# Ranking split around the first operands, bias rows over all partitions, residual transposes one step later, addresses in registers

## The chip, the cores and the metric

The kernel runs on one core of a Trainium2 chip. The metric is the device time of one execution in microseconds (us). The engines of the core are TensorE (PE in the profile, with its weight loads as PEld), VectorE (DVE), ScalarE (ACT), GpSimd (POOL) and SyncE (SP), which here only issues DMAs. They run side by side and are ordered by semaphores alone.

## What is computed

32 sequences of 64 tokens, 512 wide, go through four layers: a transformer-like block without mask (single-head attention with scores over the sequence, a projection, two MLPs, the residual, a clip to 0..1), an adapter (down to 256, GELU, up to 512, residual, layer norm, gain and shift), and both once more with other weights. The adapter's weights are chosen per sequence by its role.

```python
# block (layers 0 and 2)
q = x @ Wq; k = x @ Wk; v = x @ Wv
attn = softmax(einsum('btd,bTd->btT', q, k) * scale)
attn_out = einsum('btT,bTd->btd', attn, v) @ Wp + bp
cms_out = gelu(attn_out @ cW1 + cb1) @ cW2 + cb2 + one_hot(target_codes)
modifier = gelu(concatenate([attn_out, cms_out]) @ mW1 + mb1) @ mW2 + mb2
out = clip(x + cms_out + modifier, 0.0, 1.0)
# adapter (layers 1 and 3)
h = gelu(einsum('bsh,bhk->bsk', hidden_states, W_down[role]) + b_down[role])
y = hidden_states + einsum('bsk,bkh->bsh', h, W_up[role]) + b_up[role]
out = (y - mean) * rsqrt(var + 1e-5) * gamma[role] + beta[role]
```

## The kernel before

All matmuls are float32 split into a high and a low part: ACT makes the high part by a rounding copy (`... HI ...`), DVE the low part by a subtraction (`minus`, L1146), and PE adds three products (`product`, L543). Each engine's program is written out by hand in order; what follows is that order.

**Start.** Wq with Wk, and Wv with Wp, are multiplied once per layer, four products n = 0..3 (`operands(n)` splits their inputs, `results(n)` their outputs into `fw`). Products 0 and 1 arrive in chunks, 2 and 3 reuse the buffers. The outputs of 0 and 1 are stored to DRAM (`fused`, L352 on SP) before ACT may overwrite them with those of 2 and 3. DVE also ranks the batches by role (`rank_batches`, 40 small steps on tiles `rk` and `rc`, counted by the semaphore `ranked`), so that two sequences of one tile mostly have the same role; SP waits for the ranking, reads each batch number from the tile `order` into a register (L341) and loads x (`load_x`, L342). On DVE the ranking stands behind `operands(1)` and ahead of `operands(2)`. POOL splits the adapters' bias rows meanwhile (L482 to L488, tiles `rows_hi`, `rows_part`, `rows_raw`, `rows`), on four partitions, two per layer, where a sign per partition taken from the ranking's `rc` picks high or low part.

**Passes.** The tokens go in 2 halves of 16 sequences, each through 2 layers: passes p = 0..3. A pass is attention in two blocks of 512 tokens, the MLPs in 16 units, and the adapter over 8 tiles of 128 tokens. Only the last tile of the second half may mix two roles (`general`) and takes its products twice.

**Adapter.** Per tile i: DVE clips `acc` into `xc` (`clip`, L1504, two buffers), ACT and DVE split it (`split_x`), PE multiplies down (`front`, L795, bias row L798) and at its end transposes the residual into the bank of the up-projection (L803), after waiting for `yn_done` of tile i-3; ACT makes the GELU, PE transposes it (`turn_h`, L816), ACT and DVE split it (`split_h`), PE multiplies up on top of the residual (`adapter_up`, L828, L831). DVE takes the row statistics (L1526, L1529, L1531), POOL the power for the deviation (L523), DVE normalises into `yt` (L1541), POOL multiplies by the gain and adds the shift (L526, L528), which SP loads per tile with an address read per sequence (L358, two DMAs of 64 partitions). In layer 0 PE transposes y back (`turn_back`, L840) and ACT copies it to x; in layer 1 SP stores it (L387), again with an address read each, and loads the next half's x between. PE's step i is front(i+2), turn_h(i+1), turn_back(i-2), adapter_up(i). Tile 5's turn_back stands at the end of the pass, those of tiles 6 and 7 inside the next attention, behind its second and fourth product. The adapter's weights are split by `adapter_part` and `up_part` (three roles each) around the end of the last MLP unit, where DVE also makes the last quadrant (`make_z12`) and the last sums (`add`, L1394).

## Time and profile before

| | us |
|---|---|
| median of 3 runs | 2183.42 (2183.08 to 2183.86) |
| the profiled execution | 2183.24 |
| its span in the trace | 2181.4 |

| engine | busy us | share of the span |
|---|---|---|
| PE | 2094.2 | 96% |
| DVE | 1417.4 | 65% |
| ACT | 864.6 | 40% |
| POOL | 378.1 | 17% |

### The profile page before, as it was taken

How to read it: one execution, taken by the hardware profiler on the slowest of the kernel's cores; microseconds unless marked ns; L12 is line 12 of the kernel's file. 1: busy time of each engine (PE TensorE's matmuls, PEld its weight loads, DVE VectorE, ACT ScalarE, POOL GpSimd, SP SyncE). 2: the span in 40 equal slices, each digit the busy share in tenths (PEclk: the TensorE clock that was granted, in tenths of full speed). 3: DMA queues.
4: the chain of work that ended last, by engine and by line, in shares of the span. 5: the costliest groups of instructions: out<-in, count | busy, mean ns of one | idle time of the engine just before them, and what ended most of it. 6: DMA issues, size and time to landing. Idle time of an engine off the chain costs nothing.

```text
span 2181.4 us, 27070 instructions
## 1 busy us (share of the span) xinstructions
PE 2094.2 (96%) x9640; PEld 1729.3 (79%) x9640; DVE 1417.4 (65%) x2228; ACT 864.6 (40%) x1492; POOL 378.1 (17%) x348
## 2 busy tenths in 40 slices
PE   5999999999799999999889999999989999999996
PEld 4888888887688888888768888888867888888874
DVE  8577786557558777556646777765555777865563
ACT  4454453333245444333325444333324544433331
POOL 3011112210311102111130110212122111112204
PEclk8999999999999999999999999999999999999998
DMA  4501111223320121112451111111332012111123
GB/s 174 234 30 58 49 63 58 68 68 97 131 78 30 58 80 37 68 68 68 152 157 39 49 59 66 65 60 52 107 121 102 20 49 68 68 46 60 65 92 97
DMA packets 42402, 169.74 MB, mean 78 GB/s; under 512 B 5648, under 2 KB 9744, under 8 KB 34832
## 3 DMA queue, kind: packets, MB, share of 16 engines
q1 hardware_dynamic: 42272, 168.02, 22.7%
q8 instruction: 80, 1.31, 0.2%
q14 instruction: 50, 0.41, 0.1%
HBM read 146.99 MB, written 21.01 MB: 77 GB/s over the span
## 4 chain that ended last, share of the span: by engine, by line
PE 87%; DVE 6%; SPq 2%; issue 2%; ACT 1%; POOL 1%; DMA 1%; DVEq 0%; ACTq 0%; POOLq 0%
PE psum L543 80%; PE psum L828 1%; PE psum L640 1%; DVE acc L1394 1%; PE psum L618 1%; DVE yt L1541 1%; PE psum L803 1%; PE psum L795 1%; DVE xz L1146 1%; DVE stats L1526 1%; DVE fpart L1146 0%; ACT xz L1095 0%; DVE wup L1146 0%; PE psum L831 0%; POOL yt L526 0%
## 5 line engine op out<-in xcount | busy, mean ns | idle before, releaser
L543 PE MATMUL psum<-hs,wd 128*128 128x512 f32 x3072 | 718.2, 389 | 5.6 <-DVE acc L1394 5.6
L543 PEld LDWEIGHTS psum<-hs,wd 128*128 128x128 f32 x3072 | 576.1, 188 | 128.1 <-DVE acc L1394 7.3
L1394 DVE TENSOR_TENSOR acc<-psum,acc 128x512 f32<-128x512 f32 x448 | 291.0, 682 | 101.4 <-PE psum L543 101.2
L543 PE MATMUL psum<-cop,wsm 128*128 128x512 f32 x1416 | 354.7, 389 | 0.0
L543 PE MATMUL psum<-aop,wsm 128*128 128x512 f32 x1320 | 332.9, 389 | 0.0
L543 PE MATMUL psum<-aop,wsc 128*128 128x512 f32 x1320 | 310.7, 389 | 0.0
L543 PEld LDWEIGHTS psum<-cop,wsm 128*128 128x128 f32 x1416 | 265.8, 188 | 55.1
L543 PEld LDWEIGHTS psum<-aop,wsm 128*128 128x128 f32 x1320 | 247.8, 188 | 51.4
L543 PEld LDWEIGHTS psum<-aop,wsc 128*128 128x128 f32 x1320 | 247.5, 188 | 51.3
L1008 ACT ACTIVATE hs<-psum,bias 128x512 fp32r<-128x512 f32 x88 | 60.8, 691 | 445.4 <-PE psum L543 445.3
L1146 DVE TENSOR_TENSOR hs<-zt,hs 128x512 fp32r<-128x512 f32 x256 | 179.9, 703 | 85.5 <-ACT zt L1009 85.5
L1008 ACT ACTIVATE hs<-zt,bias 128x512 fp32r<-128x512 f32 x168 | 120.5, 717 | 229.1 <-DVE zt L1376 173.1
L1369 DVE TENSOR_TENSOR zt<-psum,zt 128x512 f32<-128x512 f32 x56 | 38.7, 692 | 184.5 <-PE psum L543 184.5
L1009 ACT ACTIVATE zt<-zt,bias 128x512 f32<-128x512 f32 x168 | 119.0, 708 | 0.0
L497 POOL TENSOR_TENSOR comb<-w1m 128x512 f32<-128x512 f32 x28 | 36.2, 1292 | 476.7 <-DMA w1m<-m_in 476.7
L1146 DVE TENSOR_TENSOR wsm<-w1m,wsm 128x512 fp32r<-128x512 f32 x156 | 107.9, 711 | 0.0
L543 PE MATMUL psum<-fw,xs 128*128 128x512 f32 x384 | 97.2, 406 | 4.7 <-DVE tq L1146 3.4
L978 ACT ACTIVATE wsm<-w1m 128x512 fp32r<-128x512 f32 x156 | 93.9, 623 | 3.7 <-POOL w1m L504 3.7
L501 POOL TENSOR_TENSOR comb<-comb,w1m 128x512 f32<-128x512 f32 x28 | 48.9, 1746 | 249.6 <-DVE wsm L1146 249.6
L497 POOL TENSOR_TENSOR comb<-w1c 128x256 f32<-128x256 f32 x28 | 20.7, 740 | 408.8 <-DMA w1c<-c_in 408.8
L543 PE MATMUL psum<-xs,fw 128*128 128x512 f32 x384 | 90.7, 395 | 0.4 <-DVE xs L1146 0.4
L543 PEld LDWEIGHTS psum<-fw,xs 128*128 128x128 f32 x384 | 73.1, 195 | 20.8 <-DVE tq L1146 3.9
(169 smaller groups left out, 2439.6 us busy)
## 6 DMA issues: line engine op xcount, KB each, us to landing
w1m<-m_in SPq DMA_DIRECT2D x32, 1024.0 KB, 4.9
w1c<-c_in SPq DMA_DIRECT2D x32, 512.0 KB, 3.5
w<-c_in SPq DMA_DIRECT2D x32, 512.0 KB, 3.5
w<-m_in SPq DMA_DIRECT2D x32, 512.0 KB, 3.5
gains<-roles_in SPq DMA_DIRECT2D x64, 256.0 KB, 3.6
fw<-fused SPq DMA_DIRECT2D x6, 2048.0 KB, 10.0
fused<-fw SPq DMA_DIRECT2D x4, 2048.0 KB, 8.2
xmid<-x SPq DMA_DIRECT2D x4, 2048.0 KB, 6.7
```

The lines of the kernel that those rows point to most:

```text
L497: nc.gpsimd.tensor_tensor(st, w_block(u, 1, 0), w_block(u, 1, 1), ALU.add).then_inc(s1_made, 1)
L501: nc.gpsimd.tensor_tensor(st, st, w_block(u, 0, 0), ALU.subtract).then_inc(s2_made, 1)
L543: mm = nc.tensor.matmul(out, lhs(a), rhs(b), start=(start and n == 0), stop=(stop and n == total - 1), skip_group_check=reopened)
L618: nc.tensor.matmul(out, tq[:, j // 2, HI, j % 2, i * P:(i + 1) * P], xs[:, :, j, tile], start=(j == 0), stop=False)
L640: nc.tensor.matmul(out, val[:, HI, v_cols], val[:, :, p_cols], start=True, stop=False)
L795: nc.tensor.matmul(out, tokens, wdn_flat[:, bass.ds(role * (2 * KC * BN) + (c * KC + k) * BN, BN)], start=(b == 0 and k == 0 and a == c), ...
L978: nc.scalar.activation(slot(u, i)[:, HI, :], w_source(u, i), ACT.Copy).then_inc(s_hi[i], 1)
L1008: nc.scalar.activation(hs[:, b, HI, m, :], h_source(h, u), ACT.Gelu, bias=b1)
L1009: nc.scalar.activation(h_raw(h), h_source(h, u), ACT.Gelu, bias=b1).then_inc(h_hi[h], 1)
L1146: return nc.vector.tensor_tensor(out, a, hi.bitcast(F32), ALU.subtract)
L1369: nc.vector.tensor_tensor(zt[:, 2, :], bank_b()[:, :], zt[:, 0, :], ALU.add).then_inc(u3_done, 1)
L1394: nc.vector.tensor_tensor(dst, d_out[o][:, :], dst, ALU.add).then_inc(acc_done, 1)
```

## The change

It has these parts.

- The ranking is cut in two: `compare_batches` (before the first operands) and `place_batches` (behind the second); the two steps for the sign and the one for parity of the partition are gone (37 steps for 40). The ids are loaded from ACT's queue, no longer SP's. The one-hot tile `oh` is built behind `results(3)`.
- The bias rows lie over all 128 partitions, 36 elements each, high and low part beside each other; POOL has two instructions for four, and SP stores them in four DMAs.
- PE's residual transposes are a step of their own, `residual(p, i+1)` behind `turn_h(i+1)`, and wait for `yn_done` of tile i-2; `xc` has a third buffer (`xct2`).
- `up_part(1)` and `up_part(2)`, `clip(0)`, `add` and `adapter_part(2)` change places around the end of the last unit.
- turn_back of tiles 5, 6, 7 stands in the next attention, behind products 0, 2 and 3.
- SP reads each batch number once per half and keeps it in a register; the gains of a tile of one role come in one DMA over 128 partitions.

```diff
-            sp.dma_start(ids[:, :], ids_in).then_inc(ids_loaded, 16)
...
             sp.wait_ge(ranked, RANKED)
+            sp.nop(nofuse=True)
+            where = []
             for j in range(NB):
-                load_x(0, j)
-            sp.wait_ge(rows_made, 4)
-            sp.dma_start(brows, rows[:, :].bitcast(F32)).then_inc(rows_stored, 16)
+                where.append(batch(0, j))
+                load_x(where[j], j)
+            sp.wait_ge(rows_made, 2)
+            for layer in range(LAYERS):
+                for part in range(2):
+                    half_rows = slice(layer * P // LAYERS, (layer + 1) * P // LAYERS)
+                    sp.dma_start(brows[layer, part].rearrange("(q n) -> q n", n=RW),
+                                 rows[half_rows, part, :].bitcast(F32)).then_inc(rows_stored, 16)
...
             def load_gains(half, layer, i):
                 sp.nop(nofuse=True)
-                for b in range(2):
+                pieces = 1 + general(half, i)
+                for b in range(pieces):
...
-            nc.gpsimd.tensor_copy(rows_hi[:, :], rows_raw[:, :]).then_inc(rows_made, 1)
+            nc.gpsimd.tensor_copy(rows[:, HI, :], rows_raw[:, :]).then_inc(rows_made, 1)
             pool.wait_ge(rows_made, 1)
-            pool.wait_ge(ranked, 3)
-            nc.gpsimd.tensor_scalar(rows_part[:, :], rows_hi[:, :].bitcast(F32), rc[0:2 * LAYERS, 1:2], None, ALU.mult).then_inc(rows_made, 1)
-            nc.gpsimd.tensor_scalar(rows_raw[:, :], rows_raw[:, :], rc[0:2 * LAYERS, 0:1], None, ALU.mult).then_inc(rows_made, 1)
-            pool.wait_ge(rows_made, 3)
-            nc.gpsimd.tensor_tensor(rows[:, :], rows_raw[:, :], rows_part[:, :], ALU.add).then_inc(rows_made, 1)
+            nc.gpsimd.tensor_tensor(rows[:, LO, :], rows_raw[:, :], rows[:, HI, :].bitcast(F32), ALU.subtract).then_inc(rows_made, 1)
...
+            def residual(p, i):
+                if i == 2:
+                    pe.wait_ge(acc_done, 8 * UNITS * (p + 1))
                 if i >= 3:
-                    pe.wait_ge(yn_done, e - 2)
+                    pe.wait_ge(yn_done, 8 * p + i - 2)
...
                         if i + 1 < TILES:
                             turn_h(p, i + 1)
+                            residual(p, i + 1)
                         if layer == 0 and 2 <= i < TILES - 1:
                             turn_back(p, half, i - 2)
                         adapter_up(p, half, i, r.pop(i))
-                    if layer == 0:
-                        turn_back(p, half, TILES - 3)
...
                     add(p, layer, last, 0, *range(KC))
-                    adapter_part(p, 2)
                     dve.wait_ge(xadd_done, NG * (p + 1))
                     dve.wait_ge(acc_done, 8 * UNITS * (p + 1) - 4)
                     clip(0)
+                    adapter_part(p, 2)
+                    split_x(0)
                     clip(1)
-                    split_x(0)
-                    up_part(p, 2)
+                    up_part(p, 1)
                     add(p, layer, last, 1, 0)
                     split_x(1)
-                    add(p, layer, last, 1, 1, 2, 3)
+                    dve.wait_ge(dn_done, 8 * UNITS * (p + 1))
                     clip(2)
                     split_x(2)
+                    up_part(p, 2)
                     split_h(0)
+                    add(p, layer, last, 1, 1, 2, 3)
```

DVE's program at the start, before (`fpart` are the split operands, `rk` and `rc` the ranking's tiles, `idf` the ids as floats):

```order
L1146 TENSOR_TENSOR fpart_61<-fraw_57,fpart_61 128x512 x8
L1146 TENSOR_TENSOR fpart_97<-fraw_80,fpart_97 128x512 x8
L1191 TENSOR_SCALAR rk<-odds,pcol 128x16
L1193 TENSOR_REDUCE rc<-rk 128x1
L1198 TENSOR_SCALAR rc<-rc 128x1
L1199 TENSOR_SCALAR rk<-srow,pcol 128x32
L1201 CAST idf<-ids 128x65
L1203 TENSOR_SCALAR rk<-idf 128x32
```

and in the changed kernel:

```order
L1203 TENSOR_SCALAR rk<-srow,pcol 128x32
L1205 CAST idf<-ids 128x65
L1207 TENSOR_SCALAR rk<-idf 128x32
L1208 TENSOR_SCALAR rk<-idf 128x32
L1210 TENSOR_TENSOR rk<-rk 128x32
L1211 TENSOR_REDUCE rc<-rk 128x1
L1212 TENSOR_REDUCE rc<-rk 128x1
L1214 TENSOR_REDUCE rc<-rk 128x1
L1215 TENSOR_SCALAR rk<-odds,rc 128x16
L1217 TENSOR_REDUCE rc<-rk 128x1
L1158 TENSOR_TENSOR fpart_61<-fraw_57,fpart_61 128x512 x8
L1158 TENSOR_TENSOR fpart_96<-fraw_79,fpart_96 128x512 x8
```

Ten steps of the ranking have moved ahead of the operands and three are gone.

PE's program in a tile of layer 0, from the end of the down-projection to the up-projection (`brow` bias rows, `xct` the clipped tile, `hgt` the GELU's output, `yt` the normalised tile), before:

```order
L798 MATMUL psum<-brow,onz 128x256
L803 MATMUL psum<-ident,xct 128x128 x4
L816 MATMUL psum<-ident,hgt 128x128 x2
L840 MATMUL psum<-ident,yt 128x128 x4
L828 REGISTER_ALU
L828 MATMUL psum<-wup,hz 128x512
```

and in the changed kernel:

```order
L806 MATMUL psum<-brow,onz 128x256
L828 MATMUL psum<-ident,hgt 128x128 x2
L816 MATMUL psum<-ident,xct 128x128 x4
L852 MATMUL psum<-ident,yt 128x128 x4
L840 REGISTER_ALU
L840 MATMUL psum<-wup,hz 128x512
```

The transposes of `xct` stand behind those of `hgt`, and belong to the tile before the one whose down-projection has just run.

SP's program in pass 1, the gains and the first store of a tile, before:

```order
L357 TENSOR_LOAD roles
L357 ISA x2
L358 ISA
L358 DMA gains<-roles_in 64x1024
L357 TENSOR_LOAD roles
L357 ISA x2
L358 ISA
L358 DMA gains<-roles_in 64x1024
L386 TENSOR_LOAD order
L386 ISA x2
L387 ISA
L387 DMA out<-yt 64x512
```

and in the changed kernel, the gains, both stores and the first loads of x:

```order
L370 TENSOR_LOAD roles
L370 ISA x2
L371 ISA
L371 DMA gains<-roles_in 128x1024
L397 DMA out<-yt 64x512 x2
L347 ISA
L347 DMA x<-x_in 128x256
L347 ISA
L347 DMA x<-x_in 128x256
```

One address read is left per tile, that of the gains; the stores and the loads of x have none.

## Rows read from the trace of the kernel before

**Rows 1.** Busy time by stretch: stretch, length, busy us (instructions) per engine, PEclk, DMA.
```profile
0.00:75.00 75.00, 51.44 (x216) 42.49 (x217) 53.40 (x82) 26.08 (x37) 22.04 (x21) 0.86 0.56 201
528.00:608.60 80.60, 68.06 (x348) 53.55 (x346) 46.51 (x82) 25.90 (x48) 26.47 (x25) 0.96 0.28 99
1051.00:1156.10 105.10, 86.97 (x432) 68.74 (x431) 55.66 (x106) 32.36 (x61) 25.84 (x25) 0.94 0.44 146
1580.00:1660.60 80.60, 70.35 (x365) 54.91 (x364) 45.82 (x81) 25.51 (x48) 27.24 (x27) 0.98 0.28 99
2103.00:2181.40 78.40, 55.74 (x286) 42.46 (x284) 39.69 (x75) 17.40 (x33) 25.97 (x26) 0.91 0.26 74
```

**Rows 2.** The same view, behind PE's long gap at the start.
```profile
51.40:60.00 8.60, 8.59 (x30) 7.00 (x31) 8.46 (x9) 0.00 (x0) 0.00 (x0) 0.78 0.39 112
```

**Rows 3.** Waits of PE, whole span: total us, times, longest us.
```profile
PE psum L803 <- DVE yt L1541: 30.5, 18, 1.9
...
PE psum L543 <- DVE acc L1394: 5.6, 4, 1.4
```

**Rows 4.** Timeline of the start: start us, us, engine, instruction, count, idle before.
```profile
21.81 6.11 POOL L485 TENSOR_SCALAR rows_part<-rows_hi,rc 4x2304 f32<-4x2304 f32 x1 [1.88 <-DVE rk L1199]
21.90 6.06 DVE L1203 TENSOR_SCALAR rk<-idf 128x32 f32<-128x32 f32 x1
...
34.40 4.74 DVE L1213 TENSOR_TENSOR rc<-rc 128x1 f32<-128x1 f32 x1
...
44.28 0.21 DVE L1188 STREAM_TRANSPOSE codes<-rk 128x32 f32<-128x32 f32 x1
...
46.18 4.48 DVE L1146 TENSOR_TENSOR fpart<-fraw,fpart 128x2048 fp32r<-128x2048 f32 x2
...
51.41 8.81 PE L543 MATMUL psum<-fpart 128*128 128x512 f32 x30 [20.89 <-DVE fw L1146]
```

**Rows 5.** Timeline before the first attention, SP and ACT.
```profile
63.33 15.88 SPq L352 DMA_DIRECT2D fused<-fw  x4
70.85 2.07 ACT L882 ACTIVATE fw<-psum 128x512 fp32r<-128x512 f32 x4 [34.64 <-DMA fused<-fw]
```

**Rows 6.** Timeline of pass 0's adapter: before its first tile, then one tile.
```profile
531.11 2.36 DVE L1146 TENSOR_TENSOR wup<-raw_u,wup 128x1024 fp32r<-128x1024 f32 x2 [0.18 <-ACT wup L1042]
...
568.08 0.70 DVE L1526 BATCH_NORM_STATS2 stats<-psum 128x6 f32<-128x512 f32 x1 [1.42 <-PE psum L831]
...
569.17 0.42 DVE L1504 TENSOR_SCALAR xct<-acc 128x512 f32<-128x512 f32 x1
...
570.89 0.80 DVE L1541 TENSOR_SCALAR yt<-psum,mv,rstd 128x512 f32<-128x512 f32 x1
571.75 0.66 PE L803 MATMUL psum<-ident,xct 128*128 128x128 f32 x4 [1.77 <-DVE yt L1541]
...
573.19 1.30 POOL L528 TENSOR_TENSOR yt<-yt,gains 128x512 f32<-128x512 f32 x1
...
578.59 0.66 PE L803 MATMUL psum<-ident,xct 128*128 128x128 f32 x4 [1.78 <-DVE yt L1541]
```

**Rows 7.** Timeline of pass 0's end, DVE and POOL at the same time.
```profile
591.45 4.62 DVE L1146 TENSOR_TENSOR xs<-x,xs 128x512 fp32r<-128x512 f32 x4
...
593.33 1.59 POOL L528 TENSOR_TENSOR yt<-yt,gains 128x512 f32<-128x512 f32 x1
```

**Rows 8.** SP in pass 1: timeline, one issue by source line, time to landing (page).
```profile
1100.70 1.85 SPq L358 DMA_DIRECT2D gains<-roles_in  x2
...
1106.34 2.57 SPq L342 DMA_DIRECT2D x<-x_in  x3
...
L387 SPq DMA_DIRECT2D out<-yt x32: 482/522/547, 1085.9 to 2178.6; - x32
...
gains<-roles_in SPq DMA_DIRECT2D x64, 256.0 KB, 3.6
```

**Rows 9.** Timeline, PE's last instruction.
```profile
2167.20 0.50 PE L831 MATMUL psum<-brow,onz 2*128 x1
```

More of the change, by code:

```diff
@@ L287, in general, with gain_loads @@
             return half == HALVES - 1 and i == TILES - 1
+        def gain_loads(p, i):
+            extra = sum(general(q // LAYERS, j) for q in range(p + 1) for j in range(i % 2, TILES if q < p else i + 1, 2))
+            return TILES // 2 * p + i // 2 + 1 + extra
         def x_chunk(k, b):
@@ L448, in one_pass @@
                             for j in range(3 * i, min(3 * i + 3, NB)):
-                                load_x(half + 1, j)
-            for half in range(HALVES):
-                for layer in range(LAYERS):
-                    one_pass(half, layer)
+                                load_x(after[j], j)
+            one_pass(0, 0, where, None)
+            sp.nop(nofuse=True)
+            after = [batch(1, j) for j in range(NB)]
+            one_pass(0, 1, where, after)
+            one_pass(1, 0, after, None)
+            one_pass(1, 1, after, None)
             for w in range(2):
@@ L848, in _ @@
                     mlps(p)
-                    r = {i: front(p, half, i) for i in range(2)}
+                    r = {0: front(p, half, 0)}
+                    residual(p, 0)
+                    r[1] = front(p, half, 1)
                     turn_h(p, 0)
@@ L913, in attention @@
                     nc.scalar.activation(tq[:, j // 2, HI, j % 2, :], t_bank[j][:, :], ACT.Copy).then_inc(t_hi, 1)
[L914 to L915 removed]
+                    if b == 0 and layer == 1 and j != 1:
+                        back(half, TILES - 4 + max(j, 1))
                 def values(i):
@@ L1139, in _ @@
                                     split_block(p + 1, half + 1, 0, 0, k)
-                    if layer == 0:
-                        back(half, TILES - 3)
         @block.vector
@@ L1165, in results @@
                     minus(fw[:, n % 2, LO, cols], fuse_bank[n % 2][c][:, :], fw[:, n % 2, HI, cols]).then_inc(fused_lo, 1)
-            def rank_batches():
-                rrow, crow, rcol = idf[:, 0:BATCHES], idf[:, BATCHES:2 * BATCHES], idf[:, 2 * BATCHES:]
-                odd_p, sign, n, c, below, odd, gap, last, lower, base, place, late, more = (rc[:, i:i + 1] for i in range(13))
-                at_s = [rc[:, 13 + i:14 + i] for i in range(3)]
-                (before, same, same_before, less, odd_row, last_row, less_last, here, there,
-                 t_order, t_role, t_code, wide, rows_of) = (rk[:, i, :] for i in range(14))
-                at_odds = odd_row[:, 0:BATCHES // 2]
-                done = 0
-                def step(instruction):
-                    nonlocal done
-                    done += 1
-                    instruction.then_inc(ranked, 1)
-                def wide_row(out, column):
-                    dve.wait_ge(ranked, done)
-                    step(nc.vector.tensor_copy(wide, column.to_broadcast([P, BATCHES])))
-                    dve.wait_ge(ranked, done)
-                    step(nc.vector.transpose(out, wide))
-                def is_odd(out, number):
-                    step(nc.vector.tensor_scalar(at_odds, odds[:, :], number, None, ALU.is_equal))
-                    dve.wait_ge(ranked, done)
-                    step(nc.vector.tensor_reduce(out, at_odds, AX_X, ALU.add))
@@ new lines, in _ @@
+            rrow, crow, rcol = idf[:, 0:BATCHES], idf[:, BATCHES:2 * BATCHES], idf[:, 2 * BATCHES:]
+            n, c, below, odd, gap, last, lower, base, place, late, more = (rc[:, i:i + 1] for i in range(11))
+            at_s = [rc[:, 11 + i:12 + i] for i in range(3)]
+            (before, same, same_before, less, odd_row, last_row, less_last, here, there,
+             t_order, t_role, t_code, wide, rows_of) = (rk[:, i, :] for i in range(14))
+            at_odds = odd_row[:, 0:BATCHES // 2]
@@ L1272, in _ @@
             results(3)
+            dve.wait_ge(consts_in, 16)
+            for layer in range(LAYERS):
+                for k in range(KC):
+                    nc.vector.tensor_scalar(oh[:, layer, k, :], codes[:, :], feat[:, k:k + 1],
+                                            bias[:, layer, CB2 + k:CB2 + k + 1], ALU.is_equal, ALU.add)
             def attention(p, layer, b):
```

110 lines of the change are left out of this document (56 added, 54 removed).

## The prediction

> **What bounds the kernel now.** I read the busy time by stretches first [rows 1]. TensorE (PE) is busy 2094 of 2181 us, so only its gaps can be won. The five stretches shown are the start, the adapter stage at the end of each pass with the attention start behind it, and the last stage with the tail. Their PE idle time is 75.0-51.4 = 23.6, 80.6-68.1 = 12.5, 105.1-87.0 = 18.1, 80.6-70.4 = 10.2 and 78.4-55.7 = 22.7 us, 87.1 us in all, the whole idle time of the span. The MLPs between them are solid matmul, and the change doesn't touch them. The clock is a second loss: the granted share is 0.96, 0.94, 0.98 and 0.91 of full speed in these stages [rows 1], and 0.78 in the first 8.6 us behind the long gap of the start [rows 2], so matmuls behind a gap run slower too. Then the waits of PE [rows 3]: 30.5 us in 18 waits of the residual transposes (L803) for a normalisation, 5.6 us in 4 waits of the last down-projection for an accumulation.
>
> **Start.** PE stands 20.9 us [rows 4] for the third pair of operands, whose low parts VectorE (DVE) can only make from 46.18, since it ranks the batches first. Three of its small steps stall, the first for 6.06 and the last for 4.74 us (5.6 between them), where a step such as the last one takes 0.21. Each lies under a GpSimd (POOL) instruction over the bias rows, 4 partitions x 2304 elements; the first began at 21.81 and ran 6.11 us, the DVE step began at 21.90 and ended 0.04 us behind it [rows 4]. So POOL holds DVE off: 16.4 us less 3x0.2 = 15.8. With the rows over 128 partitions each POOL instruction has 36 elements for 2304, and two remain for four; they run as soon as the rows have landed, before the second half of the ranking. I take them at nothing (bounds: 0 to 1.3 us each, what 512 elements cost POOL in [rows 6]). The first half of the ranking goes in front of the first operands, where DVE has nothing until its first chunk, and three of its steps go away: 13 steps of about 0.15 us unstalled, 2.0 us. The one-hot build between 44.5 and 46.2, 1.7 us, goes behind. What is left is the second half, 44.5-39.1 = 5.4 us and one step of 0.2. So DVE is free 15.8+2.0+1.7 = 19.5 us sooner, at 26.7, and PE starts at 51.4-19.5 = 31.9. The ids move from SP's queue, ahead of the first chunks, to ACT's queue, ahead of its first activation; ACT waits for a chunk anyway, so I count nothing (at best 0.4 us for the chunks, at worst as much if the ids came late).
>
> What is late next is the queue of SP. From the end of the ranking (44.5) to the first store of fused weights (63.3) it needs 18.8 us for 16 loads of x, each with an address read, and the rows' store [rows 4, 5]. That is untouched but for one nop where there were 16, and three more row stores, 0.4 us each by an estimate from SP's 0.52 us issue [rows 8]: store at 26.7+18.8+1.1 = 46.6. ACT may overwrite the first weights 7.5 us behind it [rows 5], at 54.1, and attention starts 4.1 us later, 58.2, for 75.0. PE would be through with its third and fourth product at 31.9+23.6 = 55.5, or 54 at full clock, and waits some 3 to 4 us. Gain 16.8 us; the clock costs a little behind that gap: **16.5** (bounds 13, if SP is slower by 3 us or more behind the four stores; 20, if PE's own end at 54 decides).
>
> **Adapter tiles.** The period in pass 0 is 578.59-571.75 = 6.84 us, of which PE waits 1.77 [rows 6]: front(i+2) ends with transposes into the bank that normalise(i-1) must have read, and that starts only after up(i-1). Moved behind turn_h(i+1) as residual(i+1), they need normalise(i-2), a whole tile older. PE's own work per tile is then 6.84-1.77 = 5.07 us in layer 0, and 4.7 in layer 1, where four back transposes are missing, as many as make the 0.66 us of L803, which partly overlap. The third xc buffer lets clip run on; nothing else of this costs PE anything, the number of matmuls is equal.
>
> What is late next here is DVE with POOL. DVE from up_done: statistics from 568.08, clip at 569.17, normalise ends 571.69 [rows 6], then split_h, half a tile wide, some 0.4: 4.05 us, under both. But POOL's two products on y end at 574.49, 2.8 us behind normalise [rows 6], and with a shorter period the next clip (both operands in SBUF, 0.42 us, less than the 0.70 of the statistics at the same width) falls under them. That POOL holds such a DVE instruction off is seen at the start [rows 4], and in the four splits of x that take 4.62 us, 1.15 each where 0.7 would do, under two POOL products [rows 7]. A clip that starts only when POOL ends, 2.7 us behind normalise, is followed by 2.65 us to the next normalise's end (571.69-569.17 with its wait for ACT, and a little): **5.35 us**, the bound of a tile. It lags by 0.3 (layer 0) and 0.7 us (layer 1) per tile, over the three or four tiles that still clip; buffers two tiles deep absorb part.
> The Trainium skill (SBUF — State Buffer, Who interferes with whom) calls this an exclusive lock: a DVE instruction in a two-port mode, or with two SBUF inputs against a reading GpSimd one, blocks fully, one with at most one SBUF input does not. By that rule the statistics and split_h, which read PSUM, pass and 5.35 stands; without any lock it would be 5.07 and 4.7 and some 4 us more in all. The trace agrees so far: the stalled steps above are of the first two kinds.
>
> **First tiles of a stage.** DVE did up_part(1) (half of 2.36 us, [rows 6]) before z12 and the last sums, and PE waited 1.4 us in each of four passes [rows 3]. Moved behind clip(0), it leaves 0.3. up_part(1) and (2) now stand before split_h(0); laid out by the same durations, uw_lo is full at 547.4 in pass 0's times and up(0) starts at 549.4, so the cover holds by 2 us (uncovered, it would cost what it is late).
>
> **Back transposes.** Tile 5's transposes stood at the end of the pass, where PE waited for POOL; they go into the next attention, behind its first product. There, POOL's product of tile 5 has ended by 2 us. PE meets DVE's splits of the next x instead: laid out in pass 0's times they end at about 585.0, PE is there at 582.7, and its first product needs them one by one: 1.2 us remain.
>
> **SP in pass 1.** One tile costs SP more than 8.2 us: gains from 1100.70, x loads to 1108.9 [rows 8]. That is longer than the tile, so gains and stores come late and the next attention waits, a good part of that stage's 18.1 us. Two gain loads become one, and stores and x loads keep their addresses in registers. A pair of loads takes 1.85 us to the end of the second issue of about 0.5 [rows 8]: 1.3 us with the address read, about 0.5 without. After: 1.3 + 2x0.55 + 3x0.45 = 3.8 us, under the 5.35 of a tile, so the queue keeps up. The single gain load over 128 partitions is not in the trace: at best it lands as one of 64 does, 3.6 us, at worst twice that; it is allowed (5.35x2-3.5) = 7.2 us, where 3.5 is POOL's pair and the issue. I take 4.5.
>
> **The sum.** What each stretch could give is its idle time plus the lost clock, (1-share) x length; what I find left is taken off.
> Pass 0: 12.5+3.2, left 0.3+0.2+1.0+1.2 idle and 0.2 clock: 12.8.
> Pass 1: 18.1+6.3, left 0.3+1.4+1.5 and 0.7: 20.5.
> Pass 2: 10.2+1.6, left 1.0: 10.8 (the mixed-role tile adds PE work that hides DVE).
> Pass 3: after PE's last matmul 13.7 us are left to the span's end [rows 9]. The chain there is DVE and POOL through two tiles; laid out again, with SP's last stores 1.3 us shorter, it is 11.2. So 22.7 less 11.2 and 1.2 = 10.3, and 1.4 of clock: 11.7.
> With the start: 16.5+12.8+20.5+10.8+11.7 = 72.3 us. The profiled execution took 2183.24 us (its span 2181.4), within 0.2 of the median. **2183.2-72.3 = 2111 us.**
>
> **Rivals.** (a) POOL and DVE stretch each other more. The two POOL products take 1.59 us each, not 1.30 [rows 6], where DVE works under them [rows 7]; then clip starts 3.25 behind normalise, a tile is 5.9 us, and 0.55 more in five tiles of four passes is 11 us: 2122. For it: the period falls by a quarter and they must overlap; against: in the tile only clip and one split do. (b) The stalls of the ranking are not POOL's doing, and the change doesn't do at the start what it says: the stall of 4.7 stays in the second half, those of 6.1 and 5.6 push the first operands back. The start gives 4: 2123. Against it is how exactly the pairs end together. (c) Slower: the single gain load. POOL needs it, normalise follows POOL, and so PE. Period (L+3.5)/2: at L = 10.2 us a tile is as long as before, and for the 72 us to be lost it has to be 5.35+72/28 = 7.9 us over 7 tiles of 4 passes, from L = 12.4 on; at 13 us a tile is 8.25 and the kernel takes 2192. Nothing near that is seen: 64 partitions land in 3.6. (d) Several small terms left out of the layout (a fetch stall, a late split): 2130.
>
> **Chances.** Forecast (2101 to 2117) 0.66; (a) 0.15; (b) 0.07; (d) 0.09; (c) 0.02; 0.01 for nothing at all. The range goes from the forecast's best end (start 20, no lock: 2101) to 2126, past (a) and (b). A measurement of this kernel tells 0.2% (4.4 us) from no change. Faster 0.97, same 0.01, slower 0.02.
>
> **What would show it.** Right: in the new profile no DVE step of the ranking over 0.6 us; PE's long gap at 30 us down to 1 to 2 us and a new one of 3 to 4 us before attention, ended by a fused store; a tile period of 5.1 to 5.4 us, no wait of the residual transposes, clip lengthened under POOL's products; SP under 4 us a tile in pass 1 and no POOL wait for gains; 11 us behind the last matmul. Wrong: POOL waiting for gains in every tile (c), POOL's products at 1.6 us and a period near 5.9 (a), steps of 4 us left in the ranking (b).

## The result

| | median us | runs | ratio to before |
|---|---|---|---|
| before | 2183.64 (2183.08 to 2186.73) | 4 | |
| changed | 2106.04 (2105.77 to 2106.42) | 4 | 0.9642, 95% interval 0.9625 to 0.9659 |

The change takes 77.6 us; 72.3 were forecast, and 2106 lies inside the range of 2101 to 2126. The profiled execution of the changed kernel has a span of 2103.8 us, 77.6 less than the span before, so the two traces can carry the whole sum.

To see where the time went I cut both traces at the same point of each pass: PE's first product of the MLPs, which is the first row with `aop,wsc` of the pass. Timeline of PE in the changed kernel (start us, us, engine, instruction, count), passes 0 and 1:

```profile
116.50 5.72 PE L551 MATMUL psum<-aop,wsc 128*128 128x512 f32 x24
...
625.49 5.72 PE L551 MATMUL psum<-aop,wsc 128*128 128x512 f32 x24
```

In the kernel before the same rows start at 134.43 and 657.26. Read like this, the stretch "pass 0" runs from pass 0's MLPs to pass 1's (657.26-134.43 before, 625.49-116.50 after) and holds the adapter of pass 0 and the next attention. The last cut is the end of PE's last matmul.

| stretch, us | before | after | gain | forecast |
|---|---|---|---|---|
| start | 134.4 | 116.5 | 17.9 | 16.5 |
| pass 0 | 522.8 | 509.0 | 13.8 | 12.8 |
| pass 1 | 528.5 | 506.2 | 22.3 | 20.5 |
| pass 2 | 523.3 | 511.4 | 12.0 | 10.8 |
| pass 3 with its tail | 472.4 | 460.8 | 11.6 | 11.7 |
| sum | 2181.4 | 2103.8 | 77.6 | 72.3 |

Busy time by stretches in the changed kernel (stretch, length, busy us and instructions of PE, PEld, DVE, ACT, POOL, then the granted clock, DMA share and GB/s): the start up to attention, the first stretch behind its gap, and the four adapter stages.

```profile
0.00:55.40 55.40, 48.77 (x217) 40.43 (x217) 33.81 (x71) 25.82 (x37) 3.15 (x19) 1.00 0.73 268
55.40:62.00 6.60, 6.60 (x22) 5.33 (x23) 6.38 (x16) 2.92 (x6) 0.44 (x1) 0.74 0.97 405
508.00:577.00 69.00, 67.38 (x358) 52.85 (x357) 48.69 (x83) 26.60 (x50) 26.48 (x25) 1.00 0.32 115
1020.00:1102.00 82.00, 79.62 (x428) 63.72 (x427) 57.71 (x105) 31.17 (x60) 27.59 (x25) 1.00 0.54 186
1532.00:1594.00 62.00, 61.40 (x334) 48.25 (x334) 42.98 (x76) 19.89 (x41) 27.26 (x27) 1.00 0.33 120
2038.00:2103.80 65.80, 52.62 (x281) 40.40 (x279) 39.27 (x73) 15.85 (x32) 26.87 (x26) 0.93 0.29 89
```

The windows are shorter than those of [rows 1], but outside them PE has next to no idle time in the passes: over the whole passes 0, 1 and 2, cut as in the table above, it is 1.6, 2.4 and 0.6 us, where it was 12.5, 18.1 and 10.2. The granted clock in these stages went from 0.94 to 0.98 back to 1.00, the level of 2.4 GHz. The waits of PE that matter here (total us, times, longest us); left out are 1.5 us for the identity at the very start, 0.9 and 0.2 for operands, and 0.3 in each of four passes for the first split of the adapter:

```profile
PE psum L551 <- DVE xs L1158: 5.7, 4, 4.0
...
...
PE psum L551 <- DVE acc L1402: 1.1, 4, 0.3
...
PE psum L852 <- POOL yt L536: 0.8, 1, 0.8
PE psum L828 <- DVE hz L1158: 0.4, 1, 0.4
```

The 30.5 us of [rows 3] are gone; four waits for the accumulation are 1.1 us for 5.6; the long gap of the start (20.9 us, [rows 4]) is 0.17, and a new one of 4.0 stands ahead of attention.

**The start.** Timeline of DVE, POOL, PE, SP and ACT:

```profile
17.28 0.80 POOL L496 TENSOR_TENSOR rows<-rows_raw,rows 128x36 fp32r<-128x36 f32 x1
...
18.55 0.15 DVE L1221 TENSOR_TENSOR rc<-rc 128x1 f32<-128x1 f32 x1
...
23.85 0.21 DVE L1199 STREAM_TRANSPOSE codes<-rk 128x32 f32<-128x32 f32 x1
...
25.10 17.28 SPq L347 DMA_DIRECT2D x<-x_in  x16
...
29.34 22.01 PE L551 MATMUL psum<-fpart 128*128 128x512 f32 x96 [0.17 <-DVE fw L1158]
...
44.90 15.03 SPq L364 DMA_DIRECT2D fused<-fw  x4
...
51.53 2.06 ACT L895 ACTIVATE fw<-psum 128x512 fp32r<-128x512 f32 x4 [16.66 <-DMA fused<-fw]
...
55.39 4.80 PE L551 MATMUL psum<-xs,fw 128*128 128x512 f32 x13 [4.04 <-DVE xs L1158]
```

POOL's last instruction on the rows takes 0.80 us, the second half of the ranking runs from 18.55 to 24.1 with no step over 0.4 us, and the third product starts at 29.3. Attention then waits for the chain that the prediction named: SP's 16 x loads, its store of the fused weights at 44.9, ACT's overwriting 6.6 us behind the start of that store.

**A tile.** Timeline of two tiles in pass 0:

```profile
541.30 0.81 DVE L1548 TENSOR_SCALAR yt<-psum,mv,rstd 128x512 f32<-128x512 f32 x1
...
543.61 1.28 POOL L536 TENSOR_TENSOR yt<-yt,gains 128x512 f32<-128x512 f32 x1
...
543.97 0.15 DVE L1538 TENSOR_SCALAR veps<-mv 128x1 f32<-128x1 f32 x1
544.04 1.13 DVE L1511 TENSOR_SCALAR xct<-acc 128x512 f32<-128x512 f32 x1
...
545.84 1.64 PE L840 MATMUL psum<-wup,hz 128*128 x6
...
546.47 0.81 DVE L1548 TENSOR_SCALAR yt<-psum,mv,rstd 128x512 f32<-128x512 f32 x1
...
550.85 1.64 PE L840 MATMUL psum<-wup,hz 128*128 x6
```

PE's up-projections follow each other every 5.01 us (6.84 in [rows 6]), with no wait of PE among them, while DVE's normalisations are 5.17 us apart. The clip takes 1.13 us for 0.42 [rows 6]: it begins at 544.04 under POOL's second product, which ends at 544.89, and needs 0.28 more.

**SP in pass 1.** Timeline of SP, from one tile's gains to the next:

```profile
1059.80 0.33 SPq L371 DMA_DIRECT2D gains<-roles_in  x1
1060.23 1.13 SPq L397 DMA_DIRECT2D out<-yt  x2
1061.55 1.50 SPq L347 DMA_DIRECT2D x<-x_in  x3
1064.39 0.33 SPq L371 DMA_DIRECT2D gains<-roles_in  x1
```

SP is through with a tile 3.25 us behind its first issue, and then it waits; it was over 8.2 us [rows 8]. POOL waits for gains nowhere but in the last tile of all. The page's row on the single load, with its time to landing:

```profile
gains<-roles_in SPq DMA_DIRECT2D x30, 512.0 KB, 4.1
```

### The profile page after: what moved, and what is told of

It reads as the page before. It is cut to its first block, busy times and chain, and to the rows that moved or that the text cites. A ratio compares the mean times of both kernels' runs of the same rounds, so it can differ in the third digit from the quotient of the medians.

```text
span 2103.8 us, 26741 instructions
## 1 busy us (share of the span) xinstructions
PE 2079.4 (99%) x9640; PEld 1718.6 (82%) x9640; DVE 1406.9 (67%) x2225; ACT 861.4 (41%) x1492; POOL 362.0 (17%) x346
## 4 chain that ended last, share of the span: by engine, by line
PE 92%; DVE 3%; issue 1%; SPq 1%; ACT 1%; DMA 1%; POOL 1%; ACTq 0%; DVEq 0%; POOLq 0%
PE psum L551 84%; PE psum L803 2%; PE psum L840 1%; PE psum L626 1%; PE psum L648 1%; DVE acc L1402 0%; DVE xs L1158 0%; PE psum L843 0%; SPq L333 0%; ACT wup L1056 0%; PE psum L649 0%; PE psum L628 0%; PE psum L828 0%; DMA fraw<-fuse_in 0%; PE psum L816 0%
## 5 line engine op out<-in xcount | busy, mean ns | idle before, releaser
L551 PEld LDWEIGHTS psum<-xs,fw 128*128 128x128 f32 x384 | 72.1, 191 | 23.0 <-issue 5.2
```

The source lines that it names most:

```text
L551: mm = nc.tensor.matmul(out, lhs(a), rhs(b), start=(start and n == 0), stop=(stop and n == total - 1), skip_group_check=reopened)
```

## Experiments

"Changed" below is the time of the changed kernel in the same comparison as the last four runs, 2105.28 us. The kernel before took 2185.47, 2184.17 and 2184.25 us beside the three groups of runs, so differences under 1 us between groups are not read. The third buffer of `xc` and the new places of `clip(0)`, the sums and `adapter_part(2)` were not undone by themselves. The stretches are those of the table above, each from the one profiled execution of its kernel:

| us | start | pass 0 | pass 1 | pass 2 | pass 3 | tail |
|---|---|---|---|---|---|---|
| before | 134.4 | 522.8 | 528.5 | 523.3 | 458.7 | 13.7 |
| changed | 116.5 | 509.0 | 506.2 | 511.4 | 448.2 | 12.6 |
| bias rows alone | 117.4 | 523.0 | 528.8 | 523.3 | 458.7 | 13.6 |
| residual back in front | 116.9 | 518.5 | 515.3 | 519.5 | 459.2 | 12.2 |
| SP's work as before | 115.4 | 509.0 | 526.7 | 511.4 | 448.1 | 15.2 |
| address reads only | 117.0 | 509.0 | 517.0 | 511.4 | 448.1 | 13.2 |
| up weights early | 116.6 | 510.1 | 507.3 | 512.5 | 449.3 | 11.9 |
| ranking late | 118.4 | 509.0 | 506.2 | 511.5 | 448.1 | 12.4 |
| back transposes at the end | 117.7 | 509.7 | 506.1 | 511.7 | 448.1 | 11.8 |
| POOL without the shift | 117.2 | 508.0 | 504.6 | 511.4 | 448.1 | 9.8 |
| changed, once more | 115.7 | 509.0 | 506.2 | 511.4 | 448.1 | 12.5 |
| SP's start in another order | 110.1 | 509.0 | 506.2 | 511.4 | 448.1 | 12.1 |
| tail alone | 116.0 | 509.0 | 506.2 | 511.4 | 448.1 | 9.4 |
| start and tail | 111.0 | 509.0 | 506.2 | 511.4 | 448.1 | 9.3 |

Passes repeat within 0.1 us, the start does not: nine of these executions have the changed kernel's code up to the MLPs, and reach them between 115.4 and 117.7 us. Of the kernel before, only one start was traced.

### The bias rows alone, on the kernel before

```diff
-rows_raw = at("rows_raw", [2 * LAYERS, BROW], F32, CO + 32)
+rows_raw = at("rows_raw", [P, RW], F32, CO + 32)
+rows = at("rows", [P, 2, RW], F32R, CO + 33)
...
-nc.gpsimd.tensor_copy(rows_hi[:, :], rows_raw[:, :]).then_inc(rows_made, 1)
-... rows_part, rows_raw by the sign of rc, rows by their sum
+nc.gpsimd.tensor_copy(rows[:, HI, :], rows_raw[:, :]).then_inc(rows_made, 1)
+nc.gpsimd.tensor_tensor(rows[:, LO, :], rows_raw[:, :], rows[:, HI, :].bitcast(F32), ALU.subtract).then_inc(rows_made, 1)
```

> The kernel before with one edit: the bias rows are laid over 128 partitions (36 elements each) and POOL splits them in two instructions instead of four; the order of the ranking, the tiles and SP's addresses stay. Theory (POOL's long instructions held off the small DVE steps): the three stalled steps of the ranking fall to some 0.2 us and the second operand split to what the data allow, so PE's long gap shrinks by 15.8 + 2.5 = 18 us and, since SP's loads and stores hang on the ranking too, nearly all of it arrives at the end: 17 us less, 2166 us (2164 to 2169). Rival (the stalls are not POOL's doing): the DVE steps stay at 4 to 6 us and the kernel takes 2180 to 2184 us.

Measured: 2166.03 us, ratio 0.9915 (0.9896 to 0.9935). That is 19.4 us less than the kernel before in the same comparison, whose seven runs lie between 2181.4 and 2189.0; the spans of the two traces differ by 16.6. The ranking is where it was, and its stalls are gone. Timeline of DVE, then of PE, then the busy time by stretch behind it:

```profile
19.60 0.24 DVE L1202 TENSOR_SCALAR rk<-idf 128x32 f32<-128x32 f32 x1
...
26.32 0.21 DVE L1187 STREAM_TRANSPOSE codes<-rk 128x32 f32<-128x32 f32 x1
...
33.46 24.44 PE L542 MATMUL psum<-fpart 128*128 128x512 f32 x96 [4.21 <-DVE fw L1145]
57.88 11.16 PE L542 MATMUL psum<-xs,fw 128*128 128x512 f32 x48
...
57.90:64.00 6.10, 6.10 (x27) 5.04 (x28) 4.72 (x8) 3.19 (x7) 0.43 (x1) 1.00 0.99 416
```

The step that took 6.06 us takes 0.24, and the whole ranking, 18.70 to 26.5, lasts 7.8 us. POOL's long instructions were the cause, and this one edit brings 17.0 us at the MLPs of the 17.9 that the changed kernel has there; rival (b) falls. (The edit changes the layout and also makes two instructions of four; the two were not tried apart.) There was a fourth victim, which I had not counted. Timeline of the kernel before, DVE and POOL:

```profile
16.67 4.41 DVE L1146 TENSOR_TENSOR fpart<-fraw,fpart 128x512 fp32r<-128x512 f32 x4
...
17.53 2.39 POOL L482 CAST rows_hi<-rows_raw 4x2304 fp32r<-4x2304 f32 x1 [14.51 <-DMA rows_raw<-rows_in]
...
21.00 0.22 DVE L1191 TENSOR_SCALAR rk<-odds,pcol 128x16 f32<-128x16 f32 x1
```

POOL's first instruction over the rows held back the splits of the second operands: the ranking starts at 18.70 in this run, 2.3 us sooner.

The trace also shows how little the new order of the ranking adds here. Attention starts 2.5 us later than in the changed kernel (57.9 and 55.4), but PE comes to it without a gap, and the granted clock in the next 6.1 us is 1.00, not 0.74. At 0.74 over 6.6 us PE loses 1.7 us. So of 2.5 us 0.9 are left at the MLPs (117.4 and 116.5), and 117.4 lies inside the 115.4 to 117.7 that the start moves by itself.

### The residual transposes back in front

```diff
                 mm.then_inc(dp_done, 1)
+                residual(p, i)
                 return r
...
-                    residual(p, 0)
...
-                            residual(p, i + 1)
```

> The changed kernel with the residual transposes back inside front, where they wait for the normalisation of a tile later; third buffer, ranking, gain loads and addresses stay as changed. Theory (these transposes made the tiles long): PE waits some 1.7 us for DVE's normalisation in about 18 tiles again, 30 us with some clock, 2136 us (2130 to 2142), about evenly over the four passes. Rival (the tile is bound by DVE and POOL in any case, and the place of the transposes matters little): 2108 to 2115 us.

Measured: 2146.04 us, ratio 0.9823 (0.9806 to 0.9839), 40.8 us more than the changed kernel (37.8 by the spans). Waits of PE:

```profile
PE psum L817 <- DVE yt L1547: 29.1, 18, 2.0
PE psum L551 <- DVE xs L1157: 6.9, 6, 3.7
PE psum L817 <- DVE acc L1401: 4.0, 4, 1.0
```

The count and the length of the waits are those of [rows 3], 18 and 29.1 us, so the theory holds and the rival falls. It was low by what hangs on them: the first residual transpose of a pass now waits for the last sums (4.0 us), the splits of x cost 1.2 more, and with the mean clock down from 0.997 to 0.995 of full speed PE is busy 2086.0 us with the same matmuls, for 2079.4. By stretches it is 9.5, 9.2, 8.1 and 11.0 us, the largest part of the gain in every pass but pass 1.

### SP's work as before, and the address reads alone

```diff
-                pieces = 1 + general(half, i)
+                pieces = 2
...
                     for b in range(2):
-                        sp.dma_start(out[bass.ds(where[2 * i + b], 1)] ...
+                        sp.nop(nofuse=True)
+                        sp.dma_start(out[bass.ds(batch(half, 2 * i + b), 1)] ...
...
-            after = [batch(1, j) for j in range(NB)]
+            after = [None] * NB    # load_x reads the address itself
```

> The changed kernel with SP's work as before: an address read ahead of every store and x load, and the gains in two DMAs of 64 partitions. Theory (SP's queue was longer than a tile in pass 1 and the next attention waited for it): SP needs some 8 us a tile in pass 1 against a tile of 5, and what is late there arrives at the next attention: 15 us more, 2121 us (2116 to 2126), nearly all in pass 1, under 1 us in each of the passes 0 and 2. Rival (pass 1 only gained by its tiles, SP is beside the path): 2106 to 2109 us.

> As the run before it, but the gains stay one DMA of 128 partitions, so only the address reads are back. By the same theory SP needs 8 less 0.55 = 7.4 us a tile in pass 1, still longer than 5: some 12 us more than the changed kernel, 2118 us (2112 to 2122), so the addresses carry most of it and the single gain load the rest. Rival (the gain loads carried it): under 3 us more, 2109 us.

Measured: 2128.28 us (ratio 0.9741, 0.9725 to 0.9757) with both undone, 2117.68 us (0.9689, 0.9673 to 0.9705) with the addresses alone. Pass 1 takes 20.5 and 10.9 us more, the passes 0 and 2 under 0.1, the tail 2.6 and 0.6. Timeline of SP with both undone:

```profile
1057.17 1.82 SPq L373 DMA_DIRECT2D gains<-roles_in  x2
1059.82 1.81 SPq L400 DMA_DIRECT2D out<-yt  x2
1062.39 2.55 SPq L349 DMA_DIRECT2D x<-x_in  x3
1065.77 2.21 SPq L373 DMA_DIRECT2D gains<-roles_in  x2
```

SP needs 8.6 us a tile, against a tile of PE's of 4.5. What is late reaches the others at two points. Waits of POOL in this stage and of ACT in the next attention, with both undone:

```profile
POOL yt L537 <- DMA gains<-roles_in: 25.8, 5, 5.7
ACT val L941 <- DMA out<-yt: 15.6, 1, 15.6
```

POOL waits for gains in five tiles, and ACT's first copy of the values waits until the output stores have landed; PE then stands 8.2 us in that attention (4.5 for `tq`, 2.2 for `val`, 1.5 for `soft`). The same wait of ACT is 14.8 us in the kernel before, with 8.2 us of idle PE in its attention too, 11.0 with the addresses alone and 2.8 in the changed kernel. The theory holds in place and kind; it was low in size, and wrong on the shares: I gave the addresses most of it (12 of 15), and undone first they have half (10.9 of 20.5), the second gain load the other half. I had counted that load at 0.55 us; it costs SP 1.5, 1.82 us for the pair and 0.33 for the single one.

The two large parts don't add up. In pass 1 the residual transposes cost 9.2 and SP 20.5 us, each undone with the other in place, 29.7 together; the whole change gains 22.3 there. Before, the long tiles covered much of SP's time. With the rest of the change in place, shorter tiles without SP's part gain 1.8 us in this pass (528.5 to 526.7), SP's part without the residual's new place 13.1 (to 515.3), both 22.3.

### The up weights early

```diff
                         up_part(p, 0)
+                        up_part(p, 1)
                         make_z12(p, u)
...
                     clip(1)
-                    up_part(p, 1)
```

The same on ACT.

> The changed kernel with DVE's and ACT's second part of the up weights back where it was, ahead of the last sums and the first split of the adapters. Theory of the prediction (it costs PE 1.1 us at the last down-projection in each pass): PE's wait for the accumulation grows from 0.3 to 1.4 us in four passes, 4.4 us in all, 2110.5 us. Rival (PE waits for this anyway elsewhere, for instance for the first xz or hz of the adapters): under 1.5 us, 2106 to 2107.5 us.

Measured: 2110.19 us, ratio 0.9658 (0.9645 to 0.9671), 4.9 us more. Each of the four passes is 1.1 us longer, and PE's four waits for the accumulation are 5.7 us for 1.1, as expected.

### The ranking's first half late

```diff
-            compare_batches()
             operands(0)
             operands(1)
+            compare_batches()
             place_batches()
```

> The changed kernel with the first half of the ranking back behind the second operands; the one-hot build stays late and the bias rows stay on 128 partitions. The prediction gave 2.0 us to this half: the third product's operands 2 us later, SP's queue 2 us later, so attention 2 us later, 2108 us. Rival (from the rows-only run, whose products at the MLP start came only 0.9 us after those of the changed kernel): attention is bound by SP's queue and the DMA engines, which wait for x data in any case, so under 1 us, 2106 to 2107 us.

Measured: 2107.29 us (2106.22 to 2108.35), ratio 0.9644 (0.9631 to 0.9657), 2.0 us more. PE's wait ahead of the third product is 1.57 us for 0.17, attention starts at 56.5, and the MLPs at 118.4, 0.7 above the highest of the nine executions with the changed start. The sign and size of the theory fit, but the start itself moves by 2.3 us from one execution to another, so 2 us are likely, not shown.

### The back transposes at the end of a pass

```diff
-                    if b == 0 and layer == 1 and j != 1:
-                        turn_back(p - 1, half, TILES - 4 + max(j, 1))
+                    if b == 0 and layer == 1 and j > 1:
+                        turn_back(p - 1, half, TILES - 4 + j)
...
+                    if layer == 0:
+                        turn_back(p, half, TILES - 3)
```

> The changed kernel with tile 5's back transposes at the end of the passes 0 and 2 again, not behind the first product of the next attention. Theory A: PE stands there for POOL's shift of tile 5 as it did before, and the wait comes on top: 2 us in each of two passes, 4 us, 2110 us. Theory B: the wait only takes the place of the one for DVE's splits of the next x, which stands right behind it: under 1 us in all, 2106 to 2107 us.

Measured: 2106.99 us (2105.68 to 2108.41), ratio 0.9643 (0.963 to 0.9656). Pass 0 is 0.7 and pass 2 is 0.3 us longer. Theory B: PE's waits for POOL grow by 1.5 us in two passes (0.8 to 2.3), and the splits of x that it waited for are partly done by then.

### POOL without the shift

```diff
-nc.gpsimd.tensor_tensor(y[i % 4], y[i % 4], gains[:, s, 0:V], ALU.mult).then_inc(g_done, 1)
-pool.wait_ge(g_done, e + 1)
-nc.gpsimd.tensor_tensor(y[i % 4], y[i % 4], gains[:, s, V:2 * V], ALU.add).then_inc(b_done, 1)
+nc.gpsimd.tensor_tensor(y[i % 4], y[i % 4], gains[:, s, 0:V], ALU.mult).then_inc(b_done, 1)
```

> The changed kernel without POOL's second instruction of a tile, so the adapter's added shift (beta) is left out of every tile; everything else is as changed. Theory of the prediction (POOL's two products hold clip off and set a tile of 5.35 us): clip falls from about 1.1 to 0.42 us and the tiles get shorter by 0.3 to 0.7 us, 6 us or more over the passes and 2.6 at the tail, 2098 us. Rival (the tile is PE's own work, the lag is absorbed): clip falls to 0.42 us too, but the period stays 5.01 and 4.5 us, and only the splits of x at the end of a pass (0.7 us each) and the tail (1.3 to 2.6 us) gain: 2102 us (2101 to 2104).

Measured: 2100.61 us, ratio 0.9614 (0.96 to 0.9627), 4.7 us less. This one decides the disputed bound of a tile. The clip by groups (line, engine, operation, count, then busy us and mean ns), in the changed kernel:

```profile
L1511 DVE TENSOR_SCALAR xct<-acc 128x512 f32<-128x512 f32 x32 | 18.9, 590 | 0.4
```

without the shift:

```profile
L1509 DVE TENSOR_SCALAR xct<-acc 128x512 f32<-128x512 f32 x32 | 13.4, 420 | 0.4
```

So POOL does hold the clip off, by 5.5 us over the kernel (it was 418 ns in the kernel before, where nothing lay above it). But PE's up-projections follow each other every 5.01 us in pass 0 and 4.54 in pass 1 with the shift and without it. The rival is right: the tiles are PE's. Taking the cause away shortens pass 0 by 1.0, pass 1 by 1.5, the passes 2 and 3 not at all, and the tail by 2.9. The first two are mostly waits of PE at the end of the stage: 0.8 us of the back transposes for POOL in pass 0, 0.4 for the hidden values and 0.7 for the splits of x in pass 1 are gone.

### A better start and a better tail

The start, SP's queue:

```diff
+            def store_fused(n):
+                sp.wait_ge(fused_lo, KC * (n + 1))
+                sp.dma_start(fused[n], ...).then_inc(fuse_stored[n % 2], 16)
             for j in range(NB):
+                if j == NB // 2:
+                    store_fused(0)
                 where.append(batch(0, j))
                 load_x(where[j], j)
+            store_fused(1)
             sp.wait_ge(rows_made, 2)
```

The tail, POOL and SP, in the last pass only (`root(i)` is the wait for `ve_done` and the power; it is left out at the head of the tiles 6 and 7):

```diff
+gains_end = at("gains_end", [P, 2 * V], F32, XI)    # tile 7's, loaded before the tiles
...
 nc.gpsimd.tensor_tensor(y[i % 4], y[i % 4], g[:, 0:V], ALU.mult).then_inc(g_done, 1)
+if i + 1 in early:    # tiles 6 and 7
+    root(i + 1)
 pool.wait_ge(g_done, e + 1)
 nc.gpsimd.tensor_tensor(y[i % 4], y[i % 4], g[:, V:2 * V], ALU.add).then_inc(b_done, 1)
```

> The changed kernel unchanged, to have its time beside the next three and to see how much its start moves between two profiled executions: runs with the same code up to the MLPs reached them at 115.4 to 117.7 us. 2106 us again, within 2 us.

> The changed kernel with SP's queue in another order at the start: the first store of fused weights after 8 of the 16 x loads, the second directly behind the last x load, the bias rows' stores behind it. Theory (PE's 4 us gap before attention is SP's queue, through ACT's wait for the store, and the lower clock behind it costs 1.7 us): the gap closes and the clock stays at 1.00, 5.5 us less, 2100.5 us. Rival (the x loads, now later, or DVE's splits of them become the wait): 2 us less or nothing, 2104 to 2106 us.

> The changed kernel with two edits at the very end: the last tile's gains in a buffer of their own, loaded before the tiles of the last pass, and POOL's square root of the tiles 6 and 7 ahead of its shift of the tile before. Theory (the 12.6 us behind the last matmul are a chain of POOL: shift, root, wait for DVE's normalise, product, with 0.8 us more for the late gains): laid out, POOL's last instruction ends at 2097.6 for 2100.3, 2.7 us less, 2103.3 us. Rival (SP's six last stores and their landing set the end): under 1 us less.

> Both together, the start's order of SP and the two edits of the tail. They lie 2000 us apart, so the sum of both: 8.2 us less than the changed kernel, 2098 us. Rival: the gap of the start only moves, 2102 us.

| | median us | ratio to before |
|---|---|---|
| changed, once more | 2105.28 (2104.78 to 2106.53) | 0.9642 (0.9629 to 0.9655) |
| SP's start in another order | 2099.34 (2098.69 to 2099.53) | 0.9613 (0.96 to 0.9626) |
| tail alone | 2102.69 (2101.44 to 2103.45) | 0.9629 (0.9616 to 0.9642) |
| start and tail | 2096.28 (2096.15 to 2097.08) | 0.9599 (0.9586 to 0.9612) |

The start gives 5.9 us, where 5.5 were expected. Timeline of SP, then of PE, then the busy time behind the old place of the gap:

```profile
32.65 0.43 SPq L355 DMA_DIRECT2D fused<-fw  x1
34.26 10.24 SPq L347 DMA_DIRECT2D x<-x_in  x8
44.54 0.43 SPq L355 DMA_DIRECT2D fused<-fw  x1
...
50.64 11.04 PE L558 MATMUL psum<-xs,fw 128*128 128x512 f32 x48
...
50.60:57.00 6.40, 6.40 (x30) 5.27 (x30) 4.38 (x13) 3.16 (x6) 0.00 (x0) 1.00 1.01 412
```

PE goes from the last product to attention without a wait at 1.00 of the clock, 4.75 us sooner than in the changed kernel. The last x load ends 2.1 us later than in the changed kernel (44.5 for 42.4) and is not missed. The tail gives 2.6 us by the medians and 3.1 by the traces (12.5 to 9.4); both together give 9.0, the sum within 0.5, and the fastest kernel of this study.

## Why the prediction was right, and where it was off

Each pass has the same number of matmuls in both kernels, so its gain splits into PE's idle time and PE's busy time; less busy time for the same matmuls goes with the higher granted clock. Forecast values, added up from the terms of the prediction's sum, stand in brackets:

| us | idle before | idle after | gain in idle time | gain in busy time |
|---|---|---|---|---|
| pass 0 | 12.5 | 1.6 | 10.9 (9.8) | 2.9 (3.0) |
| pass 1 | 18.1 | 2.4 | 15.7 (14.9) | 6.6 (5.6) |
| pass 2 | 10.2 | 0.6 | 9.6 (9.2) | 2.3 (1.6) |
| pass 3 to its last matmul | 9.0 | 0.6 | 8.4 (7.8) | 2.1 (1.4) |
| tail | 13.7 | 12.6 | 1.1 (2.5) | |

**Start: 17.9 for 16.5.** The cause (POOL holds DVE off) is shown by the rows-only run. The step for the third product gave 31.9 and it is 29.3: the working took the stalls inside the ranking, 15.8 us, and took the splits ahead of it as given, though POOL's first instruction lay on them; 2.3 us missed. SP's queue came out nearly as worked: 20.8 us from the ranking's end to the store, for 19.9. Attention starts at 55.4 for 58.2, and PE waits 4.0 us for it, where 3 to 4 were forecast. The clock was said to cost "a little"; it costs 1.7 us, and that is why 2.8 us more at attention are 1.4 more in the term. Since the start moves by 2.3 us from one execution to another, these 1.4 us are not clear of noise. The step on the order of the ranking is the weak one. It gave 3.7 us for the first half and the one-hot build together, and these are worth 0.9 at the MLPs, inside what the start moves by itself: PE only reaches a gap sooner.

**Tiles: the mechanism right, the bound wrong.** 5.35 us was forecast as the bound of a tile, 5.07 and 4.7 as PE's own work. Measured are 5.01 and 4.54, PE's own, below the 5.1 to 5.4 that the prediction gave as its sign. The lock of POOL on the clip is there, up to 1.30 us for 0.42, but its size was wrong. The chain in the rows of a tile above is 2.78 us from DVE's normalise (542.11) to POOL's end (544.89) and 2.39 from there to the next normalise's end (547.28), 5.17 for the 2.70 + 2.65 forecast: I let the whole clip follow POOL's end, and only its last 0.28 us do. And the 0.16 us by which a tile of DVE and POOL is longer than PE's own never hold up a tile of PE. They come out once, at the end of the stage: 0.8 us in pass 0, where the back transposes wait for POOL. In layer 1 clip and product change places: DVE comes first and POOL is held. Timeline in pass 1:

```profile
1052.58 0.42 DVE L1511 TENSOR_SCALAR xct<-acc 128x512 f32<-128x512 f32 x1
1052.64 1.49 POOL L536 TENSOR_TENSOR yt<-yt,gains 128x512 f32<-128x512 f32 x1
```

That the tiles are not bound by the lock is shown by the run without the shift. Rival (a), a tile of 5.9 us, is out. The 1.0 and 1.5 us that the sum left for the lag in pass 0 and pass 1 are close to what POOL's shift costs there by that run (1.0 and 1.5 us), but not in the way that was worked out: no tile of PE is longer for it. What these passes gained beyond the forecast (1.0 and 1.8 us) comes from elsewhere: in pass 0 from the splits of x (below), in pass 1 half from PE's waits and half from the clock, which gave back 6.6 us for 5.6. Pass 2 gained 1.2 more than forecast, 0.4 in idle time and 0.7 in busy time.

**First tiles and back transposes.** 1.1 us per pass for the up weights was right to 0.1. The back transposes were right in kind and the wait behind them was mis-sized: 1.2 us of waiting for the splits of x were to remain in pass 0, and 0.3 do. PE's other two later waits for `xs` are in pass 1, 1.4 us together, as the sum had it. The place of the transposes is worth 0.3 to 0.7 us a pass.

**SP in pass 1.** 3.8 us per tile were forecast and are 3.25. The single gain load lands after 4.1 us, for 4.5 taken and bounds of 3.6 and 7.2; rival (c) is out. That SP was "a good part" of this stage's idle time, through late gains and late stores, is shown by the two runs: undone under short tiles, SP's part costs 20.5 us of this pass.

**Pass 3: 11.6 for 11.7, by luck.** The tail gained 1.4 us less than forecast and the stage before it 1.3 more, and the two cancel. The clock term of 1.4 us there doesn't follow the rule that the prediction states, (1-share) x length, which gives 7.1 us for that window before anything is left; 2.1 were measured in busy time.

**Tail: 12.6 for 11.2.** The last tile's gains came 0.8 us too late for POOL, since their buffer comes free only with the shift of tile 5. Rows of SP and POOL:

```profile
2092.01 1.83 SPq L371 DMA_DIRECT2D gains<-roles_in  x2
...
2097.72 1.26 POOL L534 TENSOR_TENSOR yt<-yt,gains 128x512 f32<-128x512 f32 x1 [1.84 <-DMA gains<-roles_in]
```

The wait of 1.84 takes the place of the 1.06 that POOL waits in the other tiles of this stretch for DVE. The layout had not followed that load, which the last tile, the one with mixed roles, still takes in two DMAs. What the remaining 0.6 us are stays open.

**The range.** Its lower end, 2101, is called a start of 20 us and no lock. By the prediction's own numbers these are 3.5 and some 4 us beyond the forecast, 2103.4, so the range is 2 us wider there than it was worked out. The measured 2106 lies inside either.

## What to carry to other kernels

When a small step on one engine takes microseconds, look what ends with it on the engine beside: laying POOL's operand over all partitions was worth some 17 us, while what the new order of the victim's program adds to it, 0.9 us, is not clear of what the start moves by itself. Where two queues set the same stage, their parts don't add up: short tiles alone gained 1.8 us in pass 1, SP's shorter queue alone 13.1, both 22.3. And a start that is made earlier must be followed to the next thing in every queue; here the gap moved behind SP's 16 loads, and putting one store ahead of eight of them and the other ahead of the rows' stores was worth 5.9 us. Last, a term and its measured value can agree with the mechanism wrong: what POOL's shift costs a pass was forecast as longer tiles and came as waits at the end of the stage.

## What the runs showed of the chip

- On SP an x load follows the one before it 1.1 us later with an address read between them (2.55 us from the first issue to the end of the third, one issue being 0.34) and 0.58 us later without (1.50 for three). A run of them decides whether a queue keeps up with a tile of 4.5 us.
- A wait of PE of 4.0 us at the start was followed by a granted clock of 0.74 in the next 6.6 us, 1.7 us lost; in the changed kernel once more it was 0.78 in as long a stretch behind 3.9 us, and in the run with the ranking late 0.62 behind 4.0 us (with a wait of 1.6 us some 22 us earlier). So the same gap costs 1.5 to 2.5 us here. Behind the 20.9 us of the kernel before it was 0.78 over 8.6 us [rows 2], 1.9 us lost. Without a gap there it was 1.00, the level of 2.4 GHz.
- The stretch up to the MLPs, in which the DMA engines are busy for 0.73 of the time up to attention and 0.97 behind it, varies by 2.3 us between executions of the same code, while passes of some 510 us repeat within 0.1. That the load on the DMA engines is the reason is not shown.
- The hold-off between POOL and DVE works both ways. A product of POOL that starts 0.06 us behind a clip takes 1.49 us for 1.28; a clip that starts under the product ends 0.28 us behind it. DVE's 128x1 step at 543.97, one input in SBUF and one element per partition, takes 0.15 us under the same product and is not held.
